# Gelu stage of a fused convolution and expert kernel: both halves of the output product as one run of four products in one slot of eight

## The reference

```python
def _L1_ffn_ref(x, Wm, bm, expert_emb, W1, b1, W2, b2, Wo, bo):
    h = x @ Wm + bm
    t = h.reshape(bs * L_ * H, HD)                     # heads of 32
    w = jax.nn.softmax(t @ expert_emb, axis=-1)
    topw, topi = jax.lax.top_k(w, K)                   # 2 of 16
    hmid = jax.nn.gelu(jnp.einsum('td,edi->tei', t, W1) + b1, approximate=False)
    eo = jnp.einsum('tei,eio->teo', hmid, W2) + b2
    sel = jnp.take_along_axis(eo, topi[:, :, None], axis=1)
    comb = (sel * topw[:, :, None]).sum(axis=1)
    return comb.reshape(bs, L_, d) @ Wo + bo
...
    t = t + _L1_ffn_ref(_ln_t(t), ...)
```

## Time and profile before

| | us |
|---|---|
| median of 3 runs (lowest to highest) | 2293.08 (2288.99 to 2298.83) |
| profiled execution | 2290.25 |
| span of its instructions | 2288.5 |
| TensorE matmuls busy | 2019.0 (88%) |
| TensorE weight loads busy | 1146.5 (50%) |
| VectorE busy | 1331.7 (58%) |
| ScalarE busy | 1287.0 (56%) |
| GpSimd busy | 832.4 (36%) |

### The profile page before, as it was taken

The page is one execution under the profiler, slowest core; times in us unless marked ns, Lnnn a source line. Parts: engine busy times, 40 slices in busy tenths (PEclk is TensorE's granted clock), DMA queues, the critical chain, the costliest instruction groups (busy, mean ns, idle before and its releaser), DMA issues. The chain is left out here.

```text
span 2288.5 us, 35877 instructions
## 1 busy us (share of the span) xinstructions
PE 2019.0 (88%) x12850; PEld 1146.5 (50%) x12851; DVE 1331.7 (58%) x2117; ACT 1287.0 (56%) x1634; POOL 832.4 (36%) x608
## 2 busy tenths in 40 slices
PE   6999789999796776588589985999999999999998
PEld 3444355555453554477356653444444444444444
DVE  5666435555355886122278983666667666666533
ACT  2444322222254332122145533999999999999997
POOL 4333112111000677200478821444344444443443
PEclk8999859999798765799779998999999999999999
DMA  2110032211433442477523424666655666666664
GB/s 58 30 29 15 20 100 69 65 59 40 173 132 98 125 147 93 135 208 204 148 74 115 135 102 128 159 161 172 164 159 169 166 166 164 166 170 164 156 165 114
DMA packets 280562, 281.22 MB, mean 123 GB/s; under 512 B 44998, under 2 KB 261654, under 8 KB 280278
## 3 DMA queue, kind: packets, MB, share of 16 engines
q1 hardware_dynamic: 246422, 233.49, 37.1%
q0 software_dynamic: 12288, 25.72, 3.8%
q10 hardware_dynamic: 21696, 19.93, 2.6%
HBM read 203.76 MB, written 75.25 MB: 122 GB/s over the span
## 5 line engine op out<-in xcount | busy, mean ns | idle before, releaser
L2361 ACT ACTIVATE BIG<-psA,b_s 128x1024 f32<-128x1024 f32 x784 | 810.8, 1125 | 58.3 <-PE psA L2299 55.9
L2288 POOL TENSOR_TENSOR BIG<-BIG 128x1024 f32<-128x1024 f32 x147 | 362.4, 2466 | 520.8 <-DVE BIG L2382 520.8
L2299 PE MATMUL psA<-x_r,w_r 128*128 128x512 f32 x1568 | 460.0, 423 | 16.7 <-DMA x_r<-hs_d 12.3
L2382 DVE SCALAR_TENSOR_TENSOR BIG<-psA,b_s,BIG 128x512 f32<-128x512 f32 x392 | 290.6, 749 | 247.7 <-PE psA L2310 232.8
L2299 PEld LDWEIGHTS psA<-x_r,w_r 128*128 128x128 f32 x1568 | 272.3, 190 | 257.8 <-ACT BIG L2361 148.8
L2310 PE MATMUL psA<-BIG,w_s 128*32 128x512 f32 x3136 | 378.8, 600 | 0.6 <-ACT BIG L2361 0.4
L2310 PEld LDWEIGHTS psA<-BIG,w_s 128*32 128x32 f32 x3136 | 85.4, 109 | 188.7 <-issue 126.3
L719 DVE TENSOR_REDUCE b_nm<-psN 112x32 f32<-112x512 f32 x128 | 83.0, 685 | 148.3 <-PE psN L616 147.9
L1199 POOL DMA_INDIRECT xg_d<-xnb,SLOT x128 | 135.1, 1055 | 80.9 <-DVE SLOT L1314 44.3
L1777 POOL DMA_INDIRECT gath<-yg_d,SLOT x128 | 136.9, 1070 | 38.5 <-issue 36.0
L719 DVE TENSOR_REDUCE a_nm<-psN 98x32 f32<-98x512 f32 x128 | 82.3, 684 | 90.2 <-PE psN L607 90.0
(11 more groups left out here) (394 smaller groups left out, 3175.9 us busy)
## 6 DMA issues: line engine op xcount, KB each, us to landing
BIG<-wt_d SPq DMA_DIRECT2D x784, 128.0 KB, 3.3
x_r<-hs_d SPq DMA_DIRECT2D x196, 128.0 KB, 3.6
xg_d<-ex SPq DMA_DIRECT2D x64, 264.0 KB, 3.6
xv<-xg_d SPq DMA_DIRECT2D x66, 256.0 KB, 3.2
BIG<-ypad_d SPq DMA_DIRECT2D x140, 120.0 KB
xv<-x SPq DMA_DIRECT2D x64, 196.0 KB, 2.7
hs_d<-xv SPq DMA_DIRECT2D x32, 392.0 KB, 3.2
yg_d<-ex ACTq DMA_DIRECT2D x33, 256.0 KB, 3.6
```

Of the source, the lines that this page charges most:

```text
L2288: eng.tensor_tensor(gacc[:, w % 2], gacc[:, w % 2], gsum[:, a % 2], ALU.add).then_inc(Q["acc"], 1)
L2299: mm = eng.matmul(psA[FIRST_PAIR[m] % PAIRS_PS][:, b * BLK:(b + 1) * BLK], w1_r[:, m % 16], x_r[:, w % 2, b * BLK:(b + 1) * BLK], start=Tr ...
L2361: eng.activation(hid[:, m % 8], psA[FIRST_PAIR[m] % PAIRS_PS][:], ACT.Gelu, bias=b1_s[:, m % 16:m % 16 + 1]).then_inc(Q["gel"], 1)
L2382: eng.scalar_tensor_tensor(out=dst, in0=bank_pair(use)[:, b * BLK:(b + 1) * BLK], scalar=b2_s[:, g % 4:g % 4 + 1], in1=wb[:, g % 3, b * BL ...
```

## The change

The two halves of the output product of a part, which stood in two slots one behind the other, stand in the second of these two. `LAST` has one entry for a part. `last(c)` issues four products (two halves of the output channels, two halves of the input channels; eight matmul instructions) into columns 0 to 255 and 256 to 511 of its guest bank and signals once. `finish(c)` waits for that signal and does its two operations one behind the other, each behind its wait for the former store, and signals once, behind the second. SyncE issues the stores of both halves in the one slot. Folds stay where they are. Since `ROUTE` avoids the slots in `LAST`, the tables of the routing are other ones too, though no line of them is edited. For the last part the product moves from slots 199 and 200 to slot 199.

```diff
-        LAST = {8 * c + 11 + m_: (c, m_) for c in range(len(PARTS) - 1) for m_ in range(2)}
-        LAST.update({4 * NU + 3 + m_: (len(PARTS) - 1, m_) for m_ in range(2)})
+        LAST = {8 * c + 12: c for c in range(len(PARTS) - 1)}
+        LAST[4 * NU + 3] = len(PARTS) - 1
...
                     if k in LAST:
-                        c, m_ = LAST[k]
+                        c = LAST[k]
                         wait(eng, Q["got"], EXTRA_USE["last", k] + 1)
-                        for image, at_, off, n in STORES[c]:
-                            eng.dma_start(out[image, m_ * 128:(m_ + 1) * 128, at_:at_ + n],
-                                          fin[:, m_, off:off + n]).then_inc(q_st[m_], 16)
+                        for m_ in range(2):
+                            for image, at_, off, n in STORES[c]:
+                                eng.dma_start(out[image, m_ * 128:(m_ + 1) * 128, at_:at_ + n],
+                                              fin[:, m_, off:off + n]).then_inc(q_st[m_], 16)
...
-                def last(c, m_, use):
+                def last(c, use):
                     n = PARTS[c][1]
 
                     wait(eng, Q["got"], EXTRA_USE["fold", 4 * min(2 * c + 1, NU - 1) + 6] + 1)
                     wait_room(eng, use)
-                    for h in range(2):
-                        mm = eng.matmul(bank_pair(use)[:, 0:n], wo_s[:, h, m_ * 128:(m_ + 1) * 128], comb[:, h, 0:n],
-                                        start=(h == 0), stop=(h == 1))
+                    for m_ in range(2):
+                        for h in range(2):
+                            mm = eng.matmul(bank_pair(use)[:, m_ * UT:m_ * UT + n], wo_s[:, h, m_ * 128:(m_ + 1) * 128], comb[:, h, 0:n],
+                                            start=(h == 0), stop=(h == 1))
                     mm.then_inc(Q["put"], 1)
...
-                def finish(c, m_, use):
+                def finish(c, use):
                     n = PARTS[c][1]
                     wait(eng, Q["put"], use + 1)
-
-                    wait(eng, q_st[m_], stored(c))
-                    eng.scalar_tensor_tensor(out=fin[:, m_, 0:n], in0=bank_pair(use)[:, 0:n], scalar=bo_s[:, m_:m_ + 1],
-                                             in1=tokens(c)[:, m_], op0=ALU.add, op1=ALU.add).then_inc(Q["got"], 1)
+                    for m_ in range(2):
+                        wait(eng, q_st[m_], stored(c))
+                        m = eng.scalar_tensor_tensor(out=fin[:, m_, 0:n], in0=bank_pair(use)[:, m_ * UT:m_ * UT + n], scalar=bo_s[:, m_:m_ + 1],
+                                                     in1=tokens(c)[:, m_], op0=ALU.add, op1=ALU.add)
+                    m.then_inc(Q["got"], 1)
```

More of the change, by code:

```diff
@@ L2346, in _ @@
                         if e == 0 and "last" in EXTRAS[k]:
-                            last(*LAST[k], EXTRA_USE["last", k])
+                            last(LAST[k], EXTRA_USE["last", k])
                         if e == 0 and "route" in EXTRAS[k]:
@@ L2391, in combine @@
                     eng.tensor_copy(dst, src).then_inc(Q["got"], 1)
-                def finish(c, m_, use):
+                def finish(c, use):
                     n = PARTS[c][1]
                     wait(eng, Q["put"], use + 1)
-                    wait(eng, q_st[m_], stored(c))
-                    eng.scalar_tensor_tensor(out=fin[:, m_, 0:n], in0=bank_pair(use)[:, 0:n], scalar=bo_s[:, m_:m_ + 1],
-                                             in1=tokens(c)[:, m_], op0=ALU.add, op1=ALU.add).then_inc(Q["got"], 1)
+                    for m_ in range(2):
[3 more added lines that the diff above has]
+                    m.then_inc(Q["got"], 1)
                 for k in range(SLOTS):
                     if "last" in EXTRAS[k]:
-                        finish(*LAST[k], EXTRA_USE["last", k])
+                        finish(LAST[k], EXTRA_USE["last", k])
                     if "route" in EXTRAS[k]:
```

## The result

The changed kernel takes 2305.76 us (median of 20 runs, 2299.93 to 2311.38), the kernel before, run beside it, 2295.11 (20 runs, 2288.99 to 2303.84): 10.65 us more, a ratio of 1.0044 [1.0033, 1.0055]. The forecast was 2303.5, +0.45%: +10.4 on a median of 3 runs, which the 20 runs put 2.0 us higher.

The account below looks back on a forecast made before the run. The prediction took TensorE's queue of instructions without holes to bound the Gelu stage. Its terms, the largest +9.9 for the finish wait and -7.1 at the start, summed to +10.4 us on the median 2293.08: 2303.5, range 2296 to 2313.

Parts of the forecast that it names:

- A: Merged slots: the fourth `first` waits for two `finish` operations in a row, stall 0.40 a slot; +9.9 us in 23 rounds.
- D1: Slot 10 (modulo 24): the fold waits for a `weigh` delayed by stretched steps 9 and 10; 0.29 x 7, +2.0 us.
- D2: Slot 12 (modulo 24): the merged `last` waits for a `weigh` delayed by steps 12 and 13; 0.56 x 7, +3.9 us.
- G: End of the stage: both last `finish` operations run 0.36 later and two stores queue, some 0.40; +0.8 us.
- B: Routes move from slots 13 and 25 to 16 and 27 (modulo 24), replacing other plain slots; -0.6 us.
- E: Slot 17 (modulo 24): stretched step 3 behind the route's copy delays `weigh` and the fourth `first`; 0.31 x 7, +2.2 us.
- F: Start of the stage: route 2's steps no longer hold up the first `weigh`, so TensorE's idle goes; -7.1 us.
- rival in which the wait is hidden: Merged slots cost only the sum of their matmuls, no `finish` stall; +1.2 us in all, 2294.3; chance 0.08.
- rival of a fixed price for an interruption: Each interruption of TensorE's queue has a fixed price, 0.31, saved in 23 rounds; -6.6 us, 2286.5; chance 0.04.
- rival of more collisions than counted: Late `weigh`s also delay GpSimd's additions, for which folds wait; +14 us or more, 2307 to 2313; chance 0.09.
- steps 3 and 10 are not stretched: Rival: these VectorE routing steps keep their length beside GpSimd's addition; +6.2 us in all, 2299.3; chance 0.13.
- rival in which the start does not recover: Gates or the later `rt` take over the stall of slot 2; +17.5 us in all, 2310.6; chance 0.13.

Follow-up runs that it names:

- two-signal kernel: The changed kernel with each product half in its own bank of the guest pair, signalled separately to its own `finish` operation: 2298.11 us, ratio 1.0017.
- kernel with the start alone: The kernel before, with only route 2's 16 steps placed from slot 2 on, behind the first `weigh`: 2289.42 us, ratio 0.997.

## Why the prediction was right, point by point

The sum was +10.4 and the stage grew by 10.28. Every mechanism in the sum is there. That the total is right to 0.1 us is luck: A was 2.5 too high, D1 and D2 together 1.6 too low, and G 0.9 too low because of the clock at the very end, which no trace ties to the change.

| step | predicted | measured | |
|---|---|---|---|
| A, finish wait | +9.9 | +7.4 | 23 x 0.32 |
| B, routes | -0.6 | -0.6 | 4.28 at 16 and 3 |
| C, slot 9 | -0.7 | -0.7 | 4.13 to 4.02 |
| D1, fold in slot 10 | +2.0 | +2.9 | 7 x 0.42 |
| D2, `last` in slot 12 | +3.9 | +4.6 | 7 x (6.60 - 5.94) |
| E, slot 17 | +2.2 | +2.0 | 7 x 0.28, its like being 3.95 |
| F, start | -7.1 | -7.2 | 16.12 for 23.30 |
| G, end | +0.8 | +1.7 | 12.07 for 10.37 |
| sum | +10.4 | +10.1 | |

**A** named the right wait, and missed its length. The term that was mis-sized is "two operations of 0.48 with 0.01 between": they overlap, and take 0.88 together. They start when predicted, T + 4.36 (1723.16 - 1718.80) for 3.49 + 0.86 = 4.35, T being the start of the `second` that begins the slot. So the load is 0.19 late and not 0.29, and with the 0.10 for a bare load the stall is 0.29 and not 0.40; the slots say 0.30 (5.94 against 5.64 in the two-signal kernel). A slip of 0.01 a round is in the working besides: 13.95 - 13.53 is 0.42, which makes 9.7 and not 9.9. The rival in which the wait is hidden is out: slots last 5.95, not 5.65. The rival of a fixed price for an interruption is out for the output product by the two-signal kernel, whose slots are still the sum of their matmuls. Its ground, that a fold costs 0.31 more than two pitches, was not looked into. The rival of more collisions than counted is out too: outside slots 4, 10, 12, 17 and 20 and the routes' places, the slots of the changed kernel last what those of before do, to 0.02, or less.

**D1, D2.** The steps stand where the tables written out by hand put them, and are stretched to the upper bound, as the trace of before let one expect. VectorE and TensorE in slots 10 and 12, with GpSimd's addition:

```profile
1456.99 2.77 POOL L2289 TENSOR_TENSOR BIG<-BIG 128x1024 f32<-128x1024 f32 x1 [1.26 <-DVE BIG L2384]
...
1457.54 2.76 DVE L1632 TENSOR_TENSOR rt<-rt,rev 98x512 f32<-98x512 f32 x1
1460.23 1.40 DVE L2384 SCALAR_TENSOR_TENSOR BIG<-psA,b_s,BIG 128x512 f32<-128x512 f32 x2
...
1461.11 0.64 PE L2322 MATMUL psA<-BIG,fold 128*32 128x256 f32 x8 [0.34 <-DVE BIG L2384]
...
1466.65 2.77 DVE L1644 TENSOR_TENSOR rt<-rt 98x512 f32<-98x512 f32 x1
1469.34 1.40 DVE L2384 SCALAR_TENSOR_TENSOR BIG<-psA,b_s,BIG 128x512 f32<-128x512 f32 x2
...
1470.22 1.97 PE L2334 MATMUL psA<-ex,wo_s 128*128 128x256 f32 x8 [0.42 <-DVE BIG L2384]
```

L1632, 0.69 in all its 28 rows of before, takes 2.76 here, so the rival "steps 3 and 10 are not stretched" is out. The rows show more than the working used: a stretched step does not run slower, it waits. Each ends 0.55 behind the end of the addition that it met, here 1457.54 + 2.76 = 1460.30 against 1456.99 + 2.77 = 1459.76, whether it was issued 0.2 or 1.4 us into it. So what it costs is what is left of the addition, and the thing to price is when the addition ends. The half `weigh` that the guest waits for ends where predicted: T + 6.81 in both slots, for T + 6.79. But the guest starts later behind it than the 0.05 used, which was that of a load released by `finish`: 1460.23 + 0.74 = 1460.97, and the fold starts at 1461.11; 1469.34 + 0.74 = 1470.08, and the product starts at 1470.22. That is 0.14 both times (the loads start 0.11 behind). For D1, where the sum had 0.05 and no bare load, this is the 0.1 that is missing. For D2, where it had 0.05 + 0.10, the start came as predicted, but the run of eight behind the bare load takes 1.97 from first start to last end and not 1.89. Each is 0.1 in 7 slots, 1.6 together. That slot 12 lasts 6.60 for the predicted 6.61 is two errors of 0.10 that cancel, the other being A's.

That the harm lies in the place and not in the number of the stretched steps is plain from the groups of the stage. First before (1441 to 2278), then after (1441 to 2294):

```profile
L1629 DVE TENSOR_TENSOR rt<-rt,rs 98x512 f32<-98x512 f32 x27 | 39.8, 1473 | 0.0
L1636 DVE TENSOR_TENSOR rt<-rt,rs 98x512 f32<-98x512 f32 x27 | 33.9, 1256 | 0.0
L1640 DVE SCALAR_TENSOR_TENSOR rt<-rt 98x512 f32<-98x512 f32 x13 | 28.1, 2162 | 0.4
L1632 DVE TENSOR_TENSOR rt<-rt,rev 98x512 f32<-98x512 f32 x27 | 18.5, 687 | 0.5
```

```profile
L1632 DVE TENSOR_TENSOR rt<-rt,rev 98x512 f32<-98x512 f32 x27 | 44.5, 1647 | 0.5
L1640 DVE SCALAR_TENSOR_TENSOR rt<-rt 98x512 f32<-98x512 f32 x14 | 24.0, 1711 | 0.5
L1636 DVE TENSOR_TENSOR rt<-rt,rs 98x512 f32<-98x512 f32 x28 | 19.1, 682 | 0.0
L1629 DVE TENSOR_TENSOR rt<-rt,rs 98x512 f32<-98x512 f32 x27 | 18.4, 682 | 0.0
```

These four lines take 120.3 us before and 106.0 after, so fewer steps are stretched, and yet TensorE waits more. Before, seven steps of each two routes (24 slots) were stretched, but only the one that delays slot 9 ended too late for TensorE. After, four are, and three of them end too late, ahead of slots 10, 12 and 17. (The rule of the Trainium skill, "SBUF — State Buffer", "Who interferes with whom", agrees with these traces: L1629, L1632, L1636, L1640 and L1644, with two operands in SBUF, are stretched when they are issued well inside an addition; the half of the rule on one SBUF input excepts the two-port modes, which the prediction leaves out; `finish`, with one there and one in PSUM, runs beside one in all 24 full parts and has a mean of 479 ns after as it had 484 before.)

**E** is as predicted to 0.03 us a slot: L1632 stands behind the route's copy, then L1634 and `weigh`, which ends at 1708.07 + 1.40 = 1709.47, T + 7.80 for the predicted T + 7.82.

```profile
1704.48 2.39 POOL L2289 TENSOR_TENSOR BIG<-BIG 128x1024 f32<-128x1024 f32 x1 [1.16 <-DVE BIG L2384]
...
1705.11 2.31 DVE L1632 TENSOR_TENSOR rt<-rt,rev 98x512 f32<-98x512 f32 x1
1707.46 0.69 DVE L1634 TENSOR_REDUCE rs<-rt 98x32 f32<-98x512 f32 x1
1708.07 1.40 DVE L2384 SCALAR_TENSOR_TENSOR BIG<-psA,b_s,BIG 128x512 f32<-128x512 f32 x2
```

**F** came whole, and the rival in which the start does not recover is out. The first `weigh` starts 1.20 behind the first `second`, TensorE has no wait above 0.15 us from there to 1441.48, and `rt` goes out at 1424.86 behind the gates, 1.9 us later against the first `second` than before, as foreseen. Its first step stands behind the second `weigh` (1432.08) and waits for nothing:

```profile
1425.36 1.92 PE L2311 MATMUL psA<-BIG,w_s 128*32 128x512 f32 x16 [0.36 <-ACT BIG L2363]
...
1426.56 1.53 DVE L2384 SCALAR_TENSOR_TENSOR BIG<-psA,b_s,BIG 128x512 f32<-128x512 f32 x2 [18.36 <-PE psA L2311]
...
1424.86 0.42 SPq L1654 DMA_DIRECT2D rt<-ex_d  x1
```

**G** is right but for the clock. TensorE idles 3.29 us ahead of the last fold, and when the clock falls behind that differs: the fold took 0.64 before and 1.08 after, the last eight matmuls 1.54 and 2.08, together 0.98 of the 1.70. The kernel with the start alone has its halves as before and its last fold at 1.08; it takes 11.35 from the last `second` to the end where the changed kernel takes 12.07. That is 0.72 at a like clock, for the 0.8 predicted: the pair of `finish` operations ends 0.26 later than the second one did (0.61 for 0.35), and from there to the end of the span it is 2.52 in place of 2.04, for the two stores.

## What to carry to other kernels

Price a merge by the sum of its instructions and then by who is released later: the run of four products cost nothing in itself, and 0.3 us a slot only because one signal at its end released two operations one behind the other, where a single one had just fitted before. When a planner places work around the thing that you move, write out its tables for both versions and look at which neighbour each moved step gets; here that was worth -7.2 and +9.5, as much as the merge itself. And where a wait takes the place of another as soon as it is removed, spread the extra work out rather than pack it.

## What the runs showed of the hardware

- Two or three vector operations of this kind in a row (256 columns, one operand in PSUM) start 0.40 us apart though each alone takes 0.48: two take 0.88, three 1.27. A run is priced by the distance of its starts.
- A VectorE step on two SBUF operands that was issued while a GpSimd addition ran ended 0.55 us behind the end of that addition: 47 steps before, 28 after, issued 0.2 to 1.4 us into additions of 2.39 or 2.77, so their lengths run from 1.50 to 2.77. Thirteen steps of the changed kernel that were issued in the last 0.1 us of one took their usual 0.68. The other way round, an addition issued 0.2 us behind the start of such a step took 2.77 in place of 2.39, 29 times before and 57 times after.
- A weight load that VectorE released started 0.05 us behind it in most places (behind `finish` in all 23 merged slots with a fourth `first`), and 0.11 to 0.12 for the guest that waits for the first half of `weigh`. The second kind has other semaphores to wait for ahead of it in program order, and its releaser is the first of two overlapping operations and not the last of its run; which of the two is the cause wasn't tried.
- Behind the same idle time of 3.29 us TensorE's granted clock was 1.00 for the whole last fold in one execution (before: first two lines) and 0.70 on average in the products behind it; in another (after: last two lines) it was at 0.55 in the fold and at 0.50, the 1.2 GHz level, for the last products:

```profile
2283.40:2284.10 0.70, 0.62 (x16) 0.35 (x16) 0.01 (x1) 0.00 (x0) 0.00 (x0) 1.00 0.00 0
2284.50:2286.20 1.70, 1.54 (x8) 1.24 (x8) 0.42 (x3) 0.00 (x0) 0.00 (x0) 0.70 0.02 5
...
2299.50:2300.70 1.20, 1.08 (x16) 0.62 (x16) 0.00 (x1) 0.00 (x0) 0.02 (x1) 0.55 0.00 0
2301.10:2303.30 2.20, 2.08 (x8) 1.78 (x8) 0.03 (x2) 0.00 (x0) 0.00 (x0) 0.50 0.00 0
```

- The part of the kernel that no edit touched took from 1415.60 to 1430.86 us in ten executions (up to the first `second`), a scatter that is more than the whole effect of the change. A difference of two profiled executions would have given +17.9 for a change of +10.65.
